# Query sums of squares in a two-layer decoder kernel: ones as the stationary operand in four column tiles, turned by two transpositions

## The reference

```python
q = (hidden_states @ Wq + bq).reshape(b, s, NH, HD).transpose(0, 2, 1, 3)
k = (encoder_hidden_states @ Wk + bk).reshape(b, se, NKV, HD).transpose(0, 2, 1, 3)
v = (encoder_hidden_states @ Wv + bv).reshape(b, se, NKV, HD).transpose(0, 2, 1, 3)
...
q = _rmsnorm(q, qn_w)      # q * rsqrt(mean(q*q, axis=-1) + 1e-6) * qn_w
k = _rmsnorm(k, kn_w)
scores = jnp.einsum('bhsd,bhed->bhse', q, k) * scale
probs = jax.nn.softmax(scores + mask, axis=-1)
out = jnp.einsum('bhse,bhed->bhsd', probs, v)
return out @ Wo
```

## Time and profile before

| | |
|---|---|
| device time, median of 3 | 990.24 us |
| lowest of them | 990.10 us |
| profiled execution, device time | 989.49 us |
| its span, first to last instruction | 987.7 us |
| mean granted TensorE clock | 0.949 |
| instructions | 14447 |
| MATMUL, of them in the sums of squares | 5066, 512 |

### The profile page before, as it was taken

One profiled execution on the slowest core, in us unless ns is written; L12 is line 12 of the kernel. 1 busy time (PEld: TensorE's weight loads), 2 busy tenths in 40 slices (PEclk: granted clock), 3 DMA queues, 4 the chain that ended last, 5 costly groups with the idle time before them and its releaser, 6 DMA issues.

```text
span 987.7 us, 14447 instructions
## 1 busy us (share of the span) xinstructions
PE 870.5 (88%) x5066; PEld 688.7 (70%) x5066; DVE 726.7 (74%) x1735; ACT 490.4 (50%) x1249; POOL 260.3 (26%) x298
## 2 busy tenths in 40 slices
PE   5756669998989899998999999999999999999964
PEld 4534557786778667976788677876688768777742
DVE  2769857968696879787868777977877876754543
ACT  3354123555543575347542665328642575476742
POOL 0417113223152220513134211531134211310100
PEclk9868788999999999999999999999999999999985
DMA  7752100010001000010001000010000000000000
GB/s 258 247 185 96 22 11 1 12 22 1 22 1 23 0 12 22 1 22 1 22 12 22 1 12 11 11 22 1 23 1 1 1 12 1 1 2 11 11 11 11
DMA packets 37064, 28.67 MB, mean 29 GB/s; under 512 B 18688, under 2 KB 34560, under 8 KB 36608
## 3 DMA queue, kind: packets, MB, share of 16 engines
q1 hardware_dynamic: 36992, 27.74, 9.1%
HBM read 25.64 MB, written 2.10 MB: 28 GB/s over the span
## 4 chain that ended last, share of the span: by engine, by line
PE 40%; DVE 35%; ACT 11%; issue 9%; POOL 2%; DMA 1%; SPq 1%; DVEq 0%; POOLq 0%; ACTq 0%
PE bank L941 6%; PE bank L1121 5%; PE bank L1211 4%; DVE S L870 4%; ACT S L567 3%; PE bank L1128 3%; PE bank L1200 3%; PE bank L1190 2%; DVE S L877 2%; PE bank L1114 2%; PE bank L1000 2%; DVE mx L873 2%; PE bank L1001 2%; DVE amax L759 2%; DVE X L633 2%
## 5 line engine op out<-in xcount | busy, mean ns | idle before, releaser
L567 ACT ACTIVATE S<-S,mx 128x128 f32<-128x128 f32 x256 | 99.4, 392 | 59.7 <-DVE mx L873 59.4
L1121 PE MATMUL bank<-XTE,w_xq 128*128 128x256 f32 x512 | 124.1, 386 | 2.9 <-ACT QA L541 1.9
L1211 PE MATMUL bank<-w_xo,OX 128*128 128x256 f32 x512 | 116.0, 380 | 0.0
L540 ACT ACTIVATE QS<-bank,per_partition_sb 128x256 f32<-128x256 f32 x128 | 60.4, 472 | 99.3 <-PE bank L1121 97.9
L1121 PEld LDWEIGHTS bank<-XTE,w_xq 128*128 128x128 f32 x512 | 94.6, 192 | 20.3 <-ACT QA L541 5.0
L1211 PEld LDWEIGHTS bank<-w_xo,OX 128*128 128x128 f32 x512 | 95.7, 190 | 14.7 <-issue 1.9
L870 DVE SCALAR_TENSOR_TENSOR S<-bank,rq,xmask 128x128 f32<-128x128 f32 x256 | 71.7, 342 | 17.5 <-PE bank L1190 14.9
L332 POOL TENSOR_TENSOR rq<-vq,minus_half 128x8 f32<-128x8 f32 x32 | 52.4, 1639 | 119.6 <-DVE vq L843 119.6
L231 POOL TENSOR_TENSOR prod<-XTA,ccolA 128x256 f32<-128x256 f32 x96 | 63.9, 695 | 47.0 <-PE bank L1001 34.4
L1190 PEld LDWEIGHTS bank<-KTX,QA 128*128 128x128 f32 x512 | 64.6, 194 | 13.2 <-issue 10.8
L1190 PE MATMUL bank<-KTX,QA 128*128 128x128 f32 x512 | 68.4, 279 | 2.2 <-ACT OX L576 2.2
(11 more groups left out here) (219 smaller groups left out, 1864.4 us busy)
## 6 DMA issues: line engine op xcount, KB each, us to landing
xin<-in_x SPq DMA_DIRECT2D x8, 256.0 KB, 2.7
cnat<-in_ctx SPq DMA_DIRECT2D x8, 256.0 KB, 2.7
ccolA<-in_ctxT SPq DMA_DIRECT2D x32, 64.0 KB, 2.7
taps_sb<-in_taps SPq DMA_DIRECT2D x1, 2048.0 KB, 10.9
ccolE<-in_ctxT SPq DMA_DIRECT2D x16, 128.0 KB, 2.3
w_xq<-in_L_xattn_Wq SPq DMA_DIRECT2D x1, 2048.0 KB, 11.3
w_xo<-in_L_xattn_Wo SPq DMA_DIRECT2D x1, 2048.0 KB, 16.2
out_x<-X SPq DMA_DIRECT2D x8, 256.0 KB, 2.1
```

What stands on the lines that cost most here:

```text
L567: ins = nc.scalar.activation(S[:, b, seq(h)], S[:, b, seq(h)], ACT.Exp, bias=mx[:, b, h:h + 1], accum_out=sm[:, b, h:h + 1])
L1121: ins = nc.tensor.matmul(cols(EQ)[:, h], w_xq[:, k, hh * XDIM:(hh + 1) * XDIM], XTE[:, k], start=k == 0, stop=k == HALVES - 1)
L1211: ins = nc.tensor.matmul(rows(EY)[:, b], OX[:, h, b], w_xo[:, n * XGROUP + h], start=n == 0 and h == 0 and b == 0, stop=n == XKV - 1 and h ...
```

## The change

The sums over the partitions are formed the other way round. The stationary operand is now a block of 32 columns of ones, and the moving one a head's whole QS of 256 rows. Head h writes its result to the partitions 32h to 32h + 31 of EQ, so that the four products use four quarters of the array's columns (column tiles). Every partition of a quarter holds the same sums, with the rows on the free axis. ACT copies the 128 x 256 result to SBUF (into QS[:, 0], which is read by then; the new names are SSQ, `e_ssc`), and PE turns it with two transpositions of 128 x 128, one for each sequence (`turn_squares`, `e_ssT`). After that the sums stand with rows on the partitions as before, head h in the columns 32h to 32h + 31, and DVE reads one of each 32. `turn_squares` is a step of its own on PE, and the copy is a step of its own on ACT.

All five order strings are laid out anew; PE's and ACT's have 32 letters q more.

```diff
+QUARTER = P // XGROUP
...
-        KS = QS[:].rearrange("p h s -> p (h s)")
+        KS, SSQ = QS[:].rearrange("p h s -> p (h s)"), QS[:, 0]
...
+                def query_squares(n):
+                    yield
+                    act.wait_ge(sems["e_ssq"], nth(g, XKV, n))
+                    sig(nc.scalar.activation(SSQ, EQ[:, 0:GB * P], ACT.Copy), "e_ssc")
...
                 yield from queries(0, 0)
                 yield from queries(0, 1)
+                yield from query_squares(0)
...
                     yield from queries(n, 0)
                     yield from queries(n, 1)
+                    yield from query_squares(n)
...
-                    dve.wait_ge(sems["e_ssq"], nth(g, XKV, n))
+                    dve.wait_ge(sems["e_ssT"], nth(g, XKV, n))
...
-                    sig(nc.vector.tensor_scalar(vq[:, n % 2], EQ[:, 0:GB * XGROUP], 1.0 / XDIM, 1e-6, ALU.mult, ALU.add), "e_vq")
+                    sums = EQ[:, 0:GB * P].rearrange("p (m r) -> p m r", r=QUARTER)[:, :, 0]
+                    sig(nc.vector.tensor_scalar(vq[:, n % 2], sums, 1.0 / XDIM, 1e-6, ALU.mult, ALU.add), "e_vq")
...
                 def query_squares(n):
+                    for h in range(XGROUP):
+                        ins = nc.tensor.matmul(EQ[h * QUARTER:(h + 1) * QUARTER, 0:GB * P], ones[:, 0:QUARTER], QS[:, h], start=True, stop=True)
+                    sig(ins, "e_ssq")
+
+                def turn_squares(n):
+                    pe.wait_ge(sems["e_ssc"], nth(g, XKV, n))
                     for b in range(GB):
-                        for h in range(XGROUP):
-                            col = b * XGROUP + h
-                            ins = nc.tensor.matmul(EQ[:, col:col + 1], QS[:, h, seq(b)], ones[:, 0:1], start=True, stop=True)
-                    sig(ins, "e_ssq")
+                        ins = nc.tensor.transpose(EQ[:, seq(b)], SSQ[:, seq(b)], ident[:])
+                    sig(ins, "e_ssT")
...
                     query_squares(n)
+                    yield
+                    turn_squares(n)
```

Of the order strings here the end of PE's:

```diff
     "pe": (
...
-        "qcyqccqycqyxcycxqxacqyayoqxyqxaqxoqaaxqayxyqxaqyoqxaqyxaqyaqyxqaoqyxaqyxqyxaaqaaoxqyxyxyaoaxyayxaoaaa"
-        "aaaaaaaaaaa"
...
+        "qxyqxyqyxqcoqccyqcaqyxcaqcqccqyxaqcxoqcyqyxaqcyqxaqxqoqyxaqyxqyxaqoqayxqaqyaqxqyaqxaaoqayxqyxaqyaqxq"
+        "aoqyaxqyxqaqyxoqaayxqaqxayxyoxyxyoaaaaaaaaa"
```

More of the change, by code:

```diff
@@ L155, in build_decoder @@
             d_xT d_xTc d_kvr d_r d_k d_kv d_rs d_kvs d_st d_o d_mp d_q d_vp d_ve d_rstd d_n d_nTc d_y
-            e_kv e_kc e_vc e_ks e_vk e_kn e_kT e_kTc e_xT e_xTc e_q e_qc e_ssq e_vq e_rq
+            e_kv e_kc e_vc e_ks e_vk e_kn e_kT e_kTc e_xT e_xTc e_q e_qc e_ssq e_ssc e_ssT e_vq e_rq
             e_sc0 e_sc1 e_mx0 e_mx1 e_e0 e_e1 e_p0 e_p1 e_pT0 e_pT1 e_pTc0 e_pTc1 e_o0 e_o1 e_oc0 e_oc1 e_y e_u
@@ L1225 @@
     "pe": (
[L1226 to L1230, removed]
@@ L1231 @@
-        "qxqoqcayxqyaaccqcayxaqxocaqccacaqcacaaqacayqyaxaxyqxaqoqxyqxyqxyqcocxyqxycqxocqyqcqxayqxyaqcyqccxqco"
-        "qcyqccqcyqcxycxqxacqyayoqxyqxaqxoqaaxqayxyqxaqyoqxaqyxaqyaqyxqaoqyxaqyxqyxaaqaaoxqyxyxyaoaxyayxaoaaa"
-        "aaaaaaaaaaa"
+        "sassasaaasaaaaaaaaaasaqscacacaqcaaccaaccacaaacacccacacacaqqqcaqcqacqaqxcyqcqxqxqcqxqccyqcyaqycaqccyq"
+        "aacyqcaacqxaacqxaqaqaaqoqaxyoqxyqyxaqyxcqaacyqoacayqxcxqcayaqxaaaqoaacyqaccacyayqqcaqccqxyacqxacqyac"
+        "xaqoacqyxaaqxaaqxqocyqcyqxycqxqcayxacyaqxoqxoacqaccqxcyqaaqcayaycqaaqcayacaqaqcxqcaxqxoycyaqyaqxxqax"
@@ new lines @@
+        "cqcoyaqyaqyqcxqaaxqayqyacqxoqcxqaxqaqxacqyoqxaqccaqcxyqxyacqycqaacaqaacqaaqcxqcxaacqyaoyqxayqaoqxacq"
+        "xyqaxqycaqxycqxoqaaqcqxyqaaqycxqyoqaxyqxqcaqaccqcyxqayaqxoqacayqcqaaqacacaacqacaqcayxyoaayqqayqycaqc"
+        "xaqyqxcaxaoacaqxycqxyqxoqacqacaqccxqqxayqacxqcaqcacaacxayaacaaxaycqaoqxyaqyaqyqcoqcxqyaqcxyqcxyqoqca"
+        "qxyqxyqyxqcoqccyqcaqyxcaqcqccqyxaqcxoqcyqyxaqcyqxaqxqoqyxaqyxqyxaqoqayqxaqyaqxqyaqxaaoqayxqyxaqyaqxq"
+        "aoqyaxqyxqaqyxoqaayxqaqxayxyoxyxyoaaaaaaaaa"
@@ L1234 @@
     ),
     "dve": (
[L1236 to L1240, removed]
@@ L1241 @@
-        "aaqcqycaqcayxayacaxoacqcoacacyayxacxaqccacaacacaaaacaaacaacqaaaayqxyqaxqaccxyqxycqqcxoxcyoyccccqcyac"
-        "xycxcqcccqcyccqxyacqxacqyaxaaxqyqaqxayxaoyoaaqxyaxyaqaayxaaxyaqxyxyaaaoaoaaaaaaaaaaaaaa"
+        "aasassassaaasssaaaaaaaaaaaaaaaaasasassacascasaqscacaqcqaccccacaacaacacaaaaaaacccacaacacaacacaccaaaqc"
+        "qcqxcyxcccccyqacaxcxcyayacqcacacaaacacaaaacaqacaaqaaaaqqaxyaxaycacayxqyaxcaqcaqcacaayacaayaacacacaax"
+        "aacaacaacaqxayaoyccocacqacxcaxacaayccqcyqaxaqxcaqyacayacxxccacqaccqaqcacycayaxaoaaxaocaaaacaaaacaaqa"
@@ L1243 @@
+        "cayacyacxcxccqacyxaycxaaqyqaacqyaqacaxaxacqacqcqxacyxacyocaocacqayxaacyaxacaaaaacaaqacaccaaaacacacxy"
+        "qxacqyaqqxaaxcyaaqcqyqcxaaxaacaycycacqcxoacoxacyqacyaaacaaaqaaacaacacaaqaacacaqacayaqycxaccaxyayqaca"
+        "aqxcxacqacacacacaxcyxoacqcaycoaxacxqacacaaacaaaaaacaaaacaayacacyaccqxyqxayqcqacxcyxqyqcqcccycyxcaocx"
+        "acaoaqcccycxyqcxcacyqcxqyaxaqqyxayxaqaqaqaayxayxoaoaaqyxayxaqayxaayxaqaxyaxyooaaaaaaaaa"
     ),
     "act": (
-        "sssaaasasassssscaacascascacsccccccccaaaacqqcqcacccxqycqxcqxyqyccxqyqcxyccqyqxyxycqxyqxcycqaxacxyccax"
@@ L1246 @@
-        "ycqacqyqxqacyqyxcxyqxcccqyxqayaxcayxaycqyaaxcxaaqyxcqccxyxycaxacqqcxyaqaxyqcaqycyqccxqqyxcyaxyaxacqy"
-        "acxaaxqcaxaccqxycycxyyqxaaqcqacqaxycyxcqyaqycxqqyxcaaxcyqaxcayqxaayxycxaacqycxcycxyxqqxyqxyqaacacaqy"
-        "qcycxacqqyxcxayqaxyxqcayxcyacxcqaacyxaacxycyqqyqxqcxyyaacaqaxyqxcaccqqyyxxyxqxycqxyqxcycxyxyccxcqqyc"
-        "qxcyaqxyacqcyqxcyqccqyxxyaxyayqxqxaaqxyaxayxyxqyqxaqyxaqyaqxayqxyaaxyqaayxqxyxyaxyaxyayxaaaaaaaaaaaa"
-        "a"
+        "sssaasaassasssscscscascaaccacccaccccqcqqcqcaacccxqcyqxcqxqcqcayqxyaqcyqccyaqqxqxqyxycqxyqyxqcyaxacya"
@@ L1251 @@
+        "acycxcxqcacqyqcyqcxyqcqcycqxyaqxaaaxqyaaqxaacqxycxycyqxcqxyccqyaxacqcxayxaccqayqcyxycqqcqxqxyqyxyaqc"
+        "axxqacyqcxyaqyaacxyacqxyaqcqxyqcxcxaacxqayqxaqcqxyqyaccqyxcqqxqqyxcyqaxayxacxyqaqxcayqxaqcxyccaayqxq"
+        "ycxqcyqxyqcaaqcxaqyxaqyxqcayqcqcyyacaqxyqayqcaqycxaaxcaayxccxycqcxqqcqxaacyqxaqxayqcqcxacxyyqxcqyaqy"
+        "axcycxqyaqcxycqcqxycaxycxyqqcyqcxqyaaqcxyacqcqxaqyxyqxyqqxyxyxaqyxqayqxqayxayaaqxayqxaqyxqyxaqaqayxq"
+        "yxaqyxaaqyxqaxqayxyxyxyxyaaaaaaaa"
     ),
@@ L1252 @@
     "pool": (
-        "sasaaaaaaaacsqaqaacacaacaacccacaaqcaaacqcaqaccqcqcqqccaaaqoaaacqcaccqcqqacaqcoaaqacacaaqccaqcqqcaqac"
-        "coaqacaaqaaccqacqqcqcaaoqcaacaaqcaacqaqcqcqcaaoqcaaaqcacaacqqaqcqcocqcqcqccqqqaoqqaqoaa"
+        "sasaaaaaaascaqcqacaacaaacccacaqccqcaacqaacaacqqqacaqcaaacaaacqaocqcccqaqqaccqaacaaocaaqacccqqqcqaaqc"
+        "oacaaqcaaaqccacqqqqcaacqocqaaacaqaacqcaqcqcacaoqcaacqaaaaccacqqqcqcocqcqccqaqqqoaqqqaoa"
     ),
     "sp": (
-        "asasqsasassasaaqaqaaoqaaoqaaoqaaqoqoooo"
+        "assaqsasasssaaqaaaqaoaqaoqaaqoaaoqqoooo"
```

## The result

| | before | after |
|---|---|---|
| device time, median | 991.64 us | 936.4 us |
| profiled execution, device time | 989.49 us | 936.48 us |
| its span | 987.7 us | 934.7 us |
| mean granted TensorE clock | 0.949 | 0.958 |
| MATMULs and weight loads of the sums and their turning | 512 | 256 + 64 |

The ratio after/before is 0.945, 95% interval 0.9434 to 0.9466: 5.5% faster, 55 us. The 991.64 of before counts the execution of 2268.74 us among its four and is 990.24 without it; in the sets run later the kernel before took 990.9 to 991.9, so the 55 us stand within about one.

What follows compares the result with a forecast made beforehand. TensorE (PE) was taken to bound the saturated middle, latency the tail. 989.5 - 5.8 (sums on PE) + 3 (copy) - 6.0 (new order) = 980.7; with 0.75 to the median 981.4, said as 981, range 966 to 1000.

Steps and rivals of the forecast that it cites:

- The new order: Re-laid order strings: 9.7 us tail wait goes, 3.7 us FFN work moves ahead, net 6.0 us off; whole re-layout +-7 us.
- The staircase: Four ones-stationary products on PE: passes of neighbouring heads overlap in 5 steps of 0.215 us, 1.08 us a stage.
- the change of width: PE switching column width around the four products: 0 to 0.28 us a stage, taken as 0.14.
- The first rival: All four heads side by side on PE: 0.43 us for the products, stage 0.79 us, kernel 967.5 us; chance 0.17.
- The return of 0.67: Time won per PE microsecond saved in the middle: mean of chain share 0.40 and busy share 0.95.
- The rest of the path: From squares' end to scaled scores: longer by about 0.40 + 0.22 us and three handovers, hidden in the middle; 2 us left in range.
- the price of the copy: 32 PSUM copies on ACT, 0.40 us each, 12.8 us more on ACT; taken as 3 us on the end.
- the transpositions: Two transpositions a stage on PE, 0.108 us apart: 0.22 us a stage.
- the old stage at 1.71 us: Old sums of squares: 16 MATMULs a stage at 0.107 us, 1.71 us of PE, 54.7 us over 32 stages.
- the count of instructions: TensorE's instructions fall by 512 - 256 - 64 = 192, to 4874.
- the 4 us between the last output projection and group 7's transposes: Tail: group 7's FFN transposes start about 4 us behind the last output projection's end instead of 13.
- rival 3: No tail gain, or PE waits for ACT's copy: 0.8 us a stage, 26 us, kernel 1007 us; chance 0.08.

Runs made afterwards that it cites:

- old_squares_new_order: The kernel before with the new order strings, the 32 new steps' letters taken out of PE's and ACT's; old squares computed: 963.98 us, ratio 0.9718.
- the joined orders: Kernel before, old squares, one order's steps up to 500 us, then the other's: new order first 980.02 us, old order first 977.03 us.
- turn_at_once: Kernel after with transpositions directly behind the squares on PE, the copy at ACT's first place behind the squares' end: 952.83 us, ratio 0.9614.

## Why the prediction was wrong

By its own steps, in the order of their weight:

- **The new order.** "Net 6.0 us off", with +-7 for the whole re-layout. It brought 27.7 (old_squares_new_order), 21.7 more than forecast. This is the largest miss. The term was built from the only place that letters alone can price, the end. That place behaved as computed: 9.7 us of wait forecast, 13.4 - 3.8 = 9.6 found between the last projection's end and the next transposes. But the tail is only 8 of the 27.7 us. 19 came from steps further ahead: by the joined orders 11.8 in the first half and 14.9 in the second, tail included. That the strings' other differences were worth little was assumed, because no single term could be read. The term was unknown, which should have widened the range and not left it at +-7.
- **The staircase.** "I take the staircase": 1.08 us, and 0.14 for the change of width. It was 0.43 for the two waves, and 0.10 + 0.14 = 0.24 for the change of width there and back. The staircase rested on the passes of a head following each other with the next head waiting behind them; in the trace four MATMULs start within 0.02 us, then four more 0.24 us later, and with full-width operands, where nothing overlaps, the same eight take 1.73 us. The first rival had the overlap right (0.43) and the change of width 0.10 too low. PE saves 0.82 us a stage and not 0.27: 26 us instead of 8.6, worth 26.5 us of time with the overlap alone.
- **The return of 0.67.** It is no property of the machine or the kernel but of the order: 0.27 in the old order, 0.77 to 0.90 in the new. For the old one the chain's share of PE (0.40) was the nearer of the two guides and the busy share of 95% misled; the mean of the two fits neither order.
- **The rest of the path** ("that cover hides it in the middle"). In the old order this is false: DVE waited 37.5 us for the sums, and the stage made the kernel slower by 11. In the new order, where copy, transpositions and `vq` have places of their own, it holds (8.5 us). Terms of stage and re-layout were added in the prediction as if they were independent: by themselves they are +11.3 and -27.7, together -55.
- **Right:** the price of the copy (3 us forecast; doubling it cost 2.3), the transpositions (0.22 us a stage), the old stage at 1.71 us, the count of instructions, the 4 us between the last output projection and group 7's transposes, and rival 3's mechanism, which turn_at_once shows at 16.4 us.

The sum in the prediction's form with what was measured: 991.6 - 27.7 (order) - 26.5 (overlap, in that order) - 1.1 (exchange of the operands with copy and transpositions, in that order, clock included) = 936.3. It is a path from kernel to kernel and closes by construction; by another path the terms have other sizes, as the +11.3 shows.

What stays open: which waits of the old order keep 0.73 of what PE saves, and so why the new one is 27.7 us shorter. No experiment names them; the two half-orders show only that they aren't in one half. Open too is the share of the clock in the new order (an estimated 5 us).

## What to carry to other kernels

In a kernel with orders laid out by hand or by a planner, a saving is worth what the order lets through. Measure it before anything is rebuilt: leave out part of the step in question and see how much comes back (here 0.27 of it). If that is little, the order is the bound, and a change that comes with a new one has to be priced with a range as wide as the order's own slack.

Four such sums over the partitions were cheapest here with ones as the stationary operand, in column tiles side by side: 0.89 us of PE a stage with the turning, against 1.71 for one-column products and 1.95 without the overlap. Where a long run of one-column moving operands can't be avoided, it is worth trying more columns: 64 cost 0.03 us of PE a stage here (2.63 for 2.60) and kept the clock up. The round trip through ACT that the turning needs costs next to nothing where other work stands between, and 0.63 us of PE a stage where it doesn't.

## What the runs showed of the hardware that was not expected

- Four fp32 products on four quarters of the columns, two MATMULs each, run as two waves of four: 8 MATMULs of 0.39 us in 0.64 us, 0.43 us for eight more of them. Going to the narrower form costs 0.10 us and going back 0.14.
- A longer run of one-column matmuls brings the granted clock down although TensorE is 100% busy in the profile: 24 of them a stage, mean clock 0.923 and 1020.5 us; the same with 64 columns, 0.960 and 987.6 us. With 16 a stage, in the old order, the effect is 1 to 2 us in 990.
- The same 28.6 us of TensorE work are worth 7.8 us in one order of the engines' steps and 25.6 in another.
